# Three residual tiles, a root by logarithm and exponential, and a new order of projections in a two-layer graph attention kernel

## The reference

```python
h = relu(layernorm(x))                       # mean, variance, / sqrt(v + 1e-5)
q, k, v = h @ Wq + bq, h @ Wk + bk, h @ Wv + bv          # 16 heads of 32
attn = softmax(where(adj == 0, -inf, q k^T / sqrt(32)))   # per head
x = x + (attn @ v) @ Wo + bo
h = relu(layernorm(x))
alpha = (h @ wq) (h @ wk)^T                  # one head of 512
alpha = softmax(max(alpha, 0) * (adj != 0), axis=queries)
x = x + alpha @ (h @ weight)
```

## Time and profile before

| | |
|---|---|
| median of 3 runs | 1922.6 us (1919.81 to 1924.29) |
| the profiled execution | 1918.12 us, its span 1916.3 us, mean granted TensorE clock 0.99 |
| PE busy | 1779.5 us, 93% of the span |
| PEld busy | 1404.2 us, 73% |
| DVE busy | 1620.9 us, 85% |
| ACT busy | 1087.8 us, 57% |
| POOL busy | 452.0 us, 24% |
| DMA | 142.48 MB, mean 74 GB/s |
| chain that ended last, by engine | PE 50%, DVE 28%, issue 8%, DMA 6%, ACT 5% |

### The profile page before, as it was taken

How to read it: one execution, slowest core, us unless ns; L and a number is a source line. 1 busy time by engine, 2 the same in 40 slices (tenths; PEclk the granted TensorE clock), 3 DMA queues, 4 the chain that set the end, 5 groups by cost and what they waited for, 6 DMA issues and landing times.

```text
span 1916.3 us, 53466 instructions
## 1 busy us (share of the span) xinstructions
PE 1779.5 (93%) x16817; PEld 1404.2 (73%) x16817; DVE 1620.9 (85%) x4904; ACT 1087.8 (57%) x2381; POOL 452.0 (24%) x1190
## 2 busy tenths in 40 slices
PE   3789999999999999999999999999999999999986
PEld 2557777777777777777777777777777777777763
DVE  5688888988888898888888888888888888888884
ACT  2356555656565555656566565656565656656551
POOL 1022221222122222222122222212221222222111
PEclk9899999999999999999999999999999999999998
DMA  3412122222222222222222221222222222222121
GB/s 109 139 53 77 50 84 81 81 70 78 74 58 80 84 69 78 79 59 74 79 86 67 79 79 51 82 82 71 79 79 68 65 78 85 68 79 79 44 58 39
DMA packets 195401, 142.48 MB, mean 74 GB/s; under 512 B 36000, under 2 KB 167072, under 8 KB 195360
## 3 DMA queue, kind: packets, MB, share of 16 engines
q1 hardware_dynamic: 178224, 108.93, 19.9%
q10 hardware_dynamic: 17136, 33.03, 5.5%
HBM read 57.94 MB, written 16.78 MB: 39 GB/s over the span
## 4 chain that ended last, share of the span: by engine, by line
PE 50%; DVE 28%; issue 8%; DMA 6%; ACT 5%; SPq 1%; ACTq 1%; DVEq 1%; POOL 0%; POOLq 0%
PE ring L360 34%; PE turned L425 6%; DVE probs L792 6%; DMA out_dram<-x 5%; ACT probs L588 3%; PE score L410 3%; DVE probs_t_lo L800 3%; DVE x L930 2%; DVE val L891 2%; PE ring L478 2%; PE pv L443 2%; DVE work L859 2%; DVE o_sum L813 2%; DVE xa L859 2%; DVE e_lo L951 1%
## 5 line engine op out<-in xcount | busy, mean ns | idle before, releaser
L598 ACT ACTIVATE probs_t_hi<-turned 128x512 f16<-128x512 f32 x512 | 304.7, 595 | 371.5 <-PE turned L425 336.9
L588 ACT ACTIVATE probs<-probs,least 128x256 f32<-128x256 f32 x1024 | 461.3, 503 | 10.8 <-DVE least L792 10.8
L792 DVE CUSTOM_DVE_ANT_0 probs<-score,far,undo_score 128x256 f32<-128x256 f32 x1024 | 450.5, 478 | 9.6 <-DVE far L978 9.6
L1081 POOL TENSOR_TENSOR heads_out<-o_sum,o_rcp 128x64 f32<-128x64 f32 x512 | 144.6, 303 | 1150.3 <-DVE o_sum L813 1141.1
L800 DVE TENSOR_TENSOR probs_t_lo<-turned,probs_t_hi 128x512 f16<-128x512 f32 x512 | 350.3, 684 | 50.8 <-ACT probs_t_hi L598 47.3
L425 PE MATMUL turned<-ident,probs 128*128 128x128 f32 x2048 | 311.6, 275 | 42.7 <-ACT probs L588 42.7
L425 PEld LDWEIGHTS turned<-ident,probs 128*128 128x128 f32 x2048 | 244.6, 142 | 89.1 <-ACT probs L588 53.3
L410 PE MATMUL score<-stack 128*128 128x256 f16 x1024 | 197.1, 274 | 16.4 <-DMA stack<-stage 16.4
L443 PE MATMUL pv<-val,probs_t_hi 128*128 128x65 f16 x2048 | 184.7, 191 | 4.6 <-DVE o_sum L813 2.7
L445 PE MATMUL pv<-val,probs_t_lo 128*128 128x33 f16 x2048 | 178.2, 179 | 0.0
L443 PEld LDWEIGHTS pv<-val,probs_t_hi 128*128 128x128 f16 x2048 | 157.8, 97 | 11.7 <-DVE probs_t_lo L800 5.6
(11 more groups left out here) (160 smaller groups left out, 4307.8 us busy)
## 6 DMA issues: line engine op xcount, KB each, us to landing
stack<-stage SPq DMA_DIRECT2D x2048, 32.0 KB, 1.9
x<-x_dram ACTq DMA_DIRECT2D x32, 512.0 KB, 4.4
out_dram<-x SPq DMA_DIRECT2D x32, 512.0 KB, 2.9
xa<-x_dram ACTq DMA_DIRECT2D x31, 512.0 KB, 3.7
adj_in<-adj_dram SPq DMA_DIRECT2D x32, 256.0 KB, 2.9
adjt_in<-adj_t_dram SPq DMA_DIRECT2D x32, 256.0 KB, 3.0
wq_raw<-wq_dram SPq DMA_DIRECT2D x2, 512.0 KB, 6.2
wk_raw<-wk_dram SPq DMA_DIRECT2D x2, 512.0 KB, 7.9
```

The source lines that it names most:

```text
L588: last = nc.scalar.activation(probs[:, u % 2, q, :], probs[:, u % 2, q, :], ACT.Exp, bias=least[:, u % 2, q:q + 1], scale=-1.0)
L598: nc.scalar.activation(pH[:, u % 2, :, :], turned[u % 2][:].rearrange("p (k n) -> p k n", k=QT), ACT.Copy).then_inc(hi["p"], 1)
L792: last = nc.vector.tensor_tensor_reduce(out=probs[:, u % 2, q, :], in0=score[u % 2][:, q * NODES:(q + 1) * NODES], in1=far[:, q, :], scale ...
L1081: last = nc.gpsimd.tensor_tensor(dst, o_sum[:, pair % 2, q:q + 3:2, :], o_rcp[:, pair % 2, q:q + 3:2].unsqueeze(2).broadcast_to([P, 2, HEAD]),
```

## The change

- `xin` and `xo` join `x1`: ScalarE loads x of graph t into `xin` at the head of step 4 of body t; GpSimd adds the bias from `xin` into `x1` in step 1 of the next body, after the outputs of the graph before are made; VectorE adds the second layer's product from `x1` into `xo`; the store reads `xo`. SyncE issues the store a body later, between stacks 2 and 3, and the last one at the end.
- The second norm's root is made by ScalarE as exp(-0.5 ln(v + eps) + ln ROOT), and VectorE applies one Newton step, folded into three operations. The variance is aggregated right after step 4's turned low part. ScalarE asks for one activation table set at its start.
- The first norm's normalisation moves from VectorE to GpSimd, as (x + minus_mean) * rstd, with one small operation more for minus_mean; its first statistics move from step 7 to 8.
- The second softmax's low part moves from the head of step 13 to behind the mask of step 12. The last pair's sum goes ahead of step 0's turned low part.
- In the dense table `qk1` (next graph) comes in steps 11 and 13, `v0` in steps 14 and 15. Stack 1 of the next graph is issued right after its stack 0.

The diff, without the new tiles' and semaphores' declarations and with most unchanged lines left out:

```diff
@@ -19 +21 @@
-NSTEPS = (3 + 4 * NEWTON_ROUNDS, 2 + 3 * NEWTON_ROUNDS)
+NSTEPS = (4 + 4 * NEWTON_ROUNDS, 3)
+ROOT = 0.5 ** (1.0 / 3.0)
@@ -35 +38 @@
     ["al"],
-    ["v0a"],
+    ["qk1a"],
     ["hw1"],
-    ["v0b", "av0"],
-    ["av1", "qk1a"],
-    ["ot0", "qk1b"],
+    ["qk1b", "av0"],
+    ["v0a", "av1"],
+    ["v0b", "ot0"],
 ]
@@ -70 +73 @@
-STATS1, VAR1, NORM1 = (7, 9), 9, 12
+STATS1, VAR1, NORM1 = (8, 9), 9, 12
 VAR2, NORM2 = 4, 5
-X1_STEP, KEEP_STEP, FAR_STEP = 1, 3, 10
+X1_STEP, XIN_STEP, KEEP_STEP, FAR_STEP = 1, 4, 3, 10
@@ -162 +165 @@
         x1 = sb("x1", [P, QT, DIM], f32)
+        xin = sb("xin", [P, QT, DIM], f32)
+        xo = sb("xo", [P, QT, DIM], f32)
         adj_in = sb("adj_in", [P, QT, NODES], i32)
@@ -331 +340 @@
                 if cur:
-                    stack_heads(1, t)
                     stack_heads(2, t)
+                if prev and started(p - 1):
+                    store(p - 1)
+                if cur:
                     stack_heads(3, t)
...
                     stack_heads(0, n)
+                    stack_heads(1, n)
                 if nxt and not cur:
...
                             load_raw(sp, name, half)
-                if prev:
-                    sp.wait_ge(final, count(p, 2, 1))
-                    sp.dma_start(out_v[p, :, :, :], x1[:]).then_inc(stored, 16)
+            def store(b):
+                sp.wait_ge(final, count(b, 2, 1))
+                sp.dma_start(out_v[b, :, :, :], xo[:]).then_inc(stored, 16)
             sweep(sp, body)
+            store(BATCH - 1)
             sp.wait_ge(stored, 16 * BATCH)
@@ -573 +587 @@
         def _(act):
+            nc.scalar.preload_act_table_set("natural_log_exp_and_others")
             def split_high(c):
@@ -656 +672 @@
+            def root(b):
+                act.wait_ge(var_ok[1], count(b, 1, 0))
+                nc.scalar.activation(newton[1][:, 0, :], meanvar[1][:, :, 1], ACT.Ln,
+                                     bias=eps[:, 0:1]).then_inc(logged, 1)
+                act.wait_ge(logged, count(b, 1, 0))
+                nc.scalar.activation(rstd[1][:], newton[1][:, 0, :], ACT.Exp,
+                                     bias=log_root[:, 0:1], scale=-0.5).then_inc(rooted, 1)
             def second_softmax(s, b):
@@ -678 +702 @@
                 present = {-1: prev, 0: cur, 1: nxt}
-                if prev:
-                    if started(p - 1):
-                        act.wait_ge(stored, count(p - 1, 16, 15))
-                    act.dma_start(x1[:], x_v[p, :, :, :]).then_inc(x1_in, 16)
                 for s in range(HEADS):
+                    if cur and s == XIN_STEP:
+                        if prev:
+                            act.wait_ge(x1_ok, count(p, 1, 0))
+                        act.dma_start(xin[:], x_v[t, :, :, :]).then_inc(x1_in, 16)
                     if cur:
...
                         exponentials(0, t + 1)
+                    if s == VAR2 and prev:
+                        root(p)
                     if prev:
@@ -708 +734 @@
+            act.wait_ge(const_ok, 2)
             sweep(act, body)
@@ -831 +858 @@
...
+                y, a, c = rstd[1][:], newton[1][:, 1, :], newton[1][:, 2, :]
+                def step(ins, at):
                     ins.then_inc(nstep[1], 1)
+                    if at < NSTEPS[1] - 1:
+                        dve.wait_ge(nstep[1], count(b, NSTEPS[1], at))
+                dve.wait_ge(rooted, count(b, 1, 0))
+                step(nc.vector.scalar_tensor_tensor(out=a, in0=y, scalar=-1.0, in1=y,
+                                                    op0=ALU.mult, op1=ALU.mult), 0)
+                step(nc.vector.scalar_tensor_tensor(out=c, in0=meanvar[1][:, :, 1], scalar=EPS,
+                                                    in1=a, op0=ALU.add, op1=ALU.mult), 1)
+                step(nc.vector.scalar_tensor_tensor(out=y, in0=c, scalar=1.5 / ROOT, in1=y,
+                                                    op0=ALU.add, op1=ALU.mult), 2)
+            def second_normalise(b):
+                dve.wait_ge(nstep[1], count(b, NSTEPS[1], NSTEPS[1] - 1))
                 for q in range(QT):
+                    nc.vector.tensor_scalar(work[:, q, :], x1[:, q, :], meanvar[1][:, q, 0:1],
+                                            rstd[1][:, q:q + 1], ALU.subtract, ALU.mult
+                                            ).then_inc(normed[1], 1)
@@ -927 +947 @@
                     dve.wait_ge(mm["av"], count(b, 2, k))
-                    nc.vector.scalar_tensor_tensor(out=x1[:, k, :], in0=src[:],
+                    if k == 0 and started(b - 1):
+                        dve.wait_ge(stored, count(b - 1, 16, 15))
+                    nc.vector.scalar_tensor_tensor(out=xo[:, k, :], in0=src[:],
                                                    scalar=undo_final[:, 0:1], in1=x1[:, k, :],
@@ -945 +967 @@
                     nc.vector.reciprocal(l1_rcp[:], l1_sum[:]).then_inc(l1_rcped, 1)
-                if s == AL_STEP + 3:
...
+            def second_low(b):
+                dve.wait_ge(hi["e"], count(b, 1, 0))
+                for m in range(QT):
+                    last = nc.vector.scalar_tensor_tensor(
+                        out=eL[:, m, :], in0=work[:, 1, m * NODES:(m + 1) * NODES],
+                        scalar=l1_rcp[:, m:m + 1], in1=eH[:, m, :],
+                        op0=ALU.mult, op1=ALU.subtract)
+                last.then_inc(lo["e"], 1)
...
                     if prev and s == NORM2:
-                        normalise(1, x1, work, p)
+                        second_normalise(p)
                     if prev:
                         second_softmax(s, p)
+                    if s == 0 and prev:
+                        sum_parts(HEADS // 2 - 1, p)
                     if cur:
                         turned_low(s, t)
-                    if s == 0 and prev:
-                        sum_parts(HEADS // 2 - 1, p)
-                    elif s > 0 and s % 2 == 0 and cur:
+                    if s == VAR2 and prev:
+                        aggregate(1, p)
+                    if s > 0 and s % 2 == 0 and cur:
                         sum_parts(s // 2 - 1, t)
@@ -978 +1003 @@
                     if s == VAR2 and prev:
-                        aggregate(1, p)
                         reciprocal_deviation(p)
+                    if s == AL_STEP + 2 and prev:
+                        second_low(p)
                     if s in STATS1 and later:
                         first_stats(STATS1.index(s), n + 1)
-                    if s == NORM1 and cur and later:
-                        normalise(0, xa, xa, n + 1)
                     for name in DENSE[s]:
@@ -1003 +1027 @@
                             split_low(c)
-                if later and not cur:
-                    normalise(0, xa, xa, n + 1)
             for q in range(QT):
...
             step(nc.vector.memset(top[:], 0.0))
+            nc.vector.memset(eps[:], EPS).then_inc(const_ok, 1)
+            nc.vector.memset(log_root[:], math.log(ROOT)).then_inc(const_ok, 1)
             dve.wait_ge(small_in, 64)
@@ -1032 +1055 @@
             step(nc.vector.memset(tops[:], 0.0))
-            normalise(0, xa, xa, 0)
             for c in range(FIRST):
@@ -1060 +1082 @@
                 settle(pool, pool_settled)
+                step(nc.gpsimd.tensor_scalar(minus_mean[:], meanvar[0][:, :, 0], -1.0, None,
+                                             ALU.mult))
                 step(nc.gpsimd.tensor_scalar(v, meanvar[0][:, :, 1], EPS, None, ALU.add))
@@ -1069 +1093 @@
                     step(nc.gpsimd.tensor_tensor(y, y, a, ALU.mult))
+            def first_normalise(b):
+                pool.wait_ge(nstep[0], count(b, NSTEPS[0], NSTEPS[0] - 1))
+                settle(pool, pool_settled)
+                for q in range(QT):
+                    nc.gpsimd.tensor_scalar(xa[:, q, :], xa[:, q, :], minus_mean[:, q:q + 1],
+                                            rstd[0][:, q:q + 1], ALU.add, ALU.mult
+                                            ).then_inc(normed[0], 1)
@@ -1093 +1125 @@
                         norm_heads(s // 2 - 1, t)
+                    if s == NORM1 and later:
+                        first_normalise(n + 1)
                     if s == X1_STEP and prev and not started(p - 1):
...
                     if s == X1_STEP and prev:
+                        if started(p - 1):
+                            pool.wait_ge(final, count(p - 1, 2, 1))
                         pool.wait_ge(x1_in, count(p, 16, 15))
                         for q in range(QT):
-                            last = nc.gpsimd.tensor_tensor(x1[:, q, :], x1[:, q, :], out_bias[:],
+                            last = nc.gpsimd.tensor_tensor(x1[:, q, :], xin[:, q, :], out_bias[:],
                                                            ALU.add)
@@ -1121 +1157 @@
             reciprocal_deviation(0)
+            first_normalise(0)
             sweep(pool, body)
```

(29 more changed lines are left out.)

10 lines of the change are left out of this document (removed).

## The result

The changed kernel takes 1848.4 us in the median of 4 runs (1848.08 to 1853.79), against 1923.1 us for the kernel before (4 runs, 1919.81 to 1924.29). The ratio is 0.962, with a 95% interval of 0.960 to 0.964. The direction was right; the size was not.

The account below looks back on a forecast made before the run. TensorE was taken as the bound, idle 2.00 us a graph; 1.59 a graph times 30 is 47.7, plus 3.8 at the tail and 0 at the start, 51.5: 1866.6, given as 1870 by the median, range 1856 to 1895.

Parts of the forecast that it names:

- head, less the new wait: Steps 0 and 1: TensorE's wait for ScalarE's exponential, 1.24 us a graph, goes entirely; 0.22 is lost again.
- the new wait: Head of a graph: third group's product waits for the values' low part, now in step 15; 0.22 us a graph lost.
- first norm's transposes: Step 6: TensorE's wait for the values' low part, 0.51 us a graph, shrinks by 0.45 through the new root.
- last product: Step 13: second softmax's low part made a step earlier, so TensorE's 0.12 us wait a graph goes.
- the sign "under 0.1": Step 6: if the forecast is right, the xa transposes' wait falls under 0.1 us a graph.
- The root: Steps 4 and 5: VectorE's 11 Newton operations become 3, 2.08 against 0.57 us; ScalarE's two activations, 0.3 each, are free.
- The rival of table loads: ScalarE's root: two table loads of 1.28 us each time, 0.5 us a graph lost, 1905 us; chance 0.05.
- the third rival: Steps 12 and 13: GpSimd's normalisation blocks VectorE throughout, 1.2 us a graph lost, 1954 us by the median; chance 0.04.
- The start: First graphs: TensorE's stand for a stack moves to head 8, some 14 us, clock falls; gain 0, between -4 and +5.
- The tail: Program's end: 3.8 us gained, from the addition 1.6, the Newton chain 0.8, the earlier low parts 1.0 and 0.4.
- The offset: Whole kernel: 1866.6 us for a profiled execution, given as 1870 because the median of the runs lay 4.5 higher.
- the forecast's own range: Whole kernel: 1861 to 1884 us, from a residual of 0.2 to 0.8 a graph and -4 to +5 at the start.

Follow-up runs that it names:

- the first improvement: Changed kernel with VectorE's second normalisation moved from the head of step 5 into its idle time in step 4: 1833.38 us.
- the longer wait: Changed kernel with one more 128x512 copy on VectorE ahead of the values' low part in step 15: 1867.94 us.
- all three improvements: Changed kernel with second normalisation in step 4, both `v0` halves in step 14, last weights' loads ahead of the first stacks: 1812.68 us.

## Why the prediction was wrong

**The step that failed** is in its first part: "the most any reordering can win in the steady part is 2.00 us a graph". It read the ceiling from the idle column, and then priced each wait by its idle time. The account by graph, from starts of matmuls:

| | forecast | idle time gone | step length gone |
|---|---|---|---|
| head, less the new wait (steps 0, 1) | 1.02 | 1.24 - 0.19 | 1.31 |
| second norm's transposes (step 5) | none | 0.07 | 0.28 |
| first norm's transposes (step 6) | 0.45 | 0.24 | 0.24 |
| last product (step 13) | 0.12 | 0.12 | 0.26 |
| sum | 1.59 | 1.48 | 2.09 |

The first row holds the 1.67 of the head, less 0.36 for the new wait; 0.13 of it came by the moved sum. Times 30, 2.14 is 64 us, and 2.1 more lie in graph 2 alone (58.53 before, 54.30 after): from graph 1 to graph 31 the traces show 66.2 where 47.7 was forecast. That is 18.5 of the 21.6 us missed. A wait that is shortened (step 6, 0.66 to 0.41 above the pitch) gives back its idle time and no more; one that vanishes gives its fixed part too (steps 0 and 13). The runs bear this out one at a time: 0.50 for 0.27, 0.35 for 0.19, and 0.59 for 0.59 where nothing vanished.

**Step 6** came out as the forecast's chain said, and still left a wait. The values' low part was forecast for 940.2 on the clock of before. In the changed kernel it ends at 906.89 + 0.68 = 907.57, and step 5 begins 32.65 us earlier there (902.06 for 934.71): 940.22. But TensorE arrives 0.28 earlier, since the unlisted wait in step 5 is gone. The other 0.13 of the 0.41 that it stands there over the pitch were in the forecast's own rows: it let TensorE arrive at 940.39, the listed end of the last matmul, where the pitch gives 940.24, and start with the low part's end, where it starts 0.15 later. So the sign "under 0.1" for this wait failed, at 0.27.

```profile
906.89 0.68 DVE L911 TENSOR_TENSOR val<-ring,val 128x512 f16<-128x512 f32 x1
```

**The root** went as forecast: two activations of 0.30 each (0.3 assumed), then VectorE's three, done at 902.63; and then VectorE stands idle for ScalarE.

```profile
901.02 0.30 ACT L677 ACTIVATE newton<-meanvar,eps 128x2 f32<-128x2 f32 x1 [0.43 <-DVE meanvar L850]
901.35 0.30 ACT L680 ACTIVATE rstd<-newton,log_root 128x2 f32<-128x2 f32 x1
...
902.91 0.47 ACT L643 ACTIVATE stage<-ring,bias_q 128x256 f16<-128x256 f32 x1 [1.27 <-PE score L424]
```

```profile
902.47 0.16 DVE L873 SCALAR_TENSOR_TENSOR rstd<-newton,rstd 128x2 f32<-128x2 f32 x1
903.78 0.48 DVE L902 SCALAR_TENSOR_TENSOR stage<-ring,bias_q,stage 128x256 f16<-128x256 f32 x1 [1.16 <-ACT stage L645]
```

The rival of table loads is dead: the two activations stand 0.33 apart, with no load between them, and the group of table loads holds one in the whole execution:

```profile
L590 ACT ACT_TABLE_LOAD x1 | 1.3, 1283 | 0.7 <-PEq L1185 0.7
```

The 1.16 us at 903.78 is what the forecast left lying, and the first improvement uses it.

**GpSimd** was costed at 1.7 us for a 128x512 normalisation. It takes 0.76:

```profile
929.42 2.14 POOL L1155 TENSOR_SCALAR far_next<-adj_in 128x256 bf16<-128x256 int32 x2
931.53 0.81 POOL L1113 TENSOR_TENSOR heads_out<-o_sum,o_rcp 128x64 f32<-128x64 f32 x2
932.33 1.51 POOL L1101 TENSOR_SCALAR xa<-xa,minus_mean,rstd 128x512 f32<-128x512 f32 x2
```

The rows it was estimated from were a two-operand addition (1.27) and a conversion from int32, and neither is near. VectorE's low part beside it took 0.88 for two, as before, while GpSimd's scaling took 0.81 where it takes 0.54 alone:

```profile
931.06 0.88 DVE L974 SCALAR_TENSOR_TENSOR e_lo<-work,l_rcp,e_hi 128x256 f16<-128x256 f32 x2
```

So GpSimd waits and VectorE does not, in this pairing: the third rival falls. The Trainium skill ("SBUF — State Buffer", on the shared port pair) lets whoever starts first have the ports, and the other blocks until it is through. The trace agrees for the scaling, which started second and took longer. It does not agree for the low part, which started at 931.06 while GpSimd's conversion ran until 931.56, and took 0.48 for the first half (0.47 in the kernel before) and not 0.5 more. With the softmax's low part given back to step 13 it does meet GpSimd's normalisation: VectorE's two then took 0.94, and GpSimd's two 1.93 in place of 1.51. GpSimd paid the most there too, and VectorE 0.06.

```profile
990.88 0.94 DVE L974 SCALAR_TENSOR_TENSOR e_lo<-work,l_rcp,e_hi 128x256 f16<-128x256 f32 x2
```

```profile
990.37 1.93 POOL L1101 TENSOR_SCALAR xa<-xa,minus_mean,rstd 128x512 f32<-128x512 f32 x2
```

**The start** came out as worked out. The stand moved from head 4 to head 8:

```profile
77.38 0.61 PE L424 MATMUL score<-stack 128*128 128x256 f16 x2 [10.95 <-DMA stack<-stage]
...
70.00:80.00 10.00, 2.62 (x19) 2.50 (x20) 3.29 (x9) 0.60 (x1) 0.54 (x2) 0.53 0.57 164
```

It is 10.95 us where 14 was said, ends at 77.4 where 75.4 was said, and the clock is granted at 0.53 in the ten microseconds around it, close to the lower level of 1.2 GHz. The gain up to step 13 of graph 1 is 0.9 us, inside -4 to +5; in the changed kernel's second profile it is -1.2, so it can't be told from nothing.

**The tail** was said to give 3.8 and gave 2.3: 0.74 in step 13 of the last graph (1.0 forecast) and 1.6 behind it (2.8). Its last 24 output products took 7.03 us where the kernel before took 5.64. The stretch from 1807 to 1815 is granted 0.79; the kernel before has 1.00 in 1875 to 1882. The fall is not a property of the changed tail: the same products took 6.50 in its second profile, and 5.64 in that of the longer wait, whose tail has the same code. So 1.4 of the 1.5 us missed here came with the execution that was profiled. Why the clock falls in one and not in another stays open.

```profile
1808.31 0.63 PE L374 MATMUL ring<-wo_lo,heads_t_hi 128*128 128x512 f16 x1
1808.73 0.63 PE L374 MATMUL ring<-wo_hi,heads_t_lo 128*128 128x512 f16 x1
```

**The offset.** The profiled execution of before lay 4.5 us under the median, and 3.4 of that went into the forecast. That of after lies at its median (1848.75 and 1848.43), so those 3.4 us were error too.

**The range.** By its own terms (0.2 to 0.8 a graph, -4 to +5 at the start) the forecast's own range is 1859 to 1886, not 1861 to 1884. That changes nothing: 1848.4 lies outside either.

## What to carry to other kernels

Price a wait of TensorE from start to start of its matmuls, less their usual pitch in a stream; the idle column leaves out the drain in front and the refill behind, here 0.15 to 0.25 us that are paid once per wait, and waits of 0.07 and 0.12 us of idle, or of none, are in no table. So look for starts that come later than the pitch, and for an end on another engine 0.15 us before them; count a ceiling from the pitch; taking away the last 0.2 us of a wait is worth more than the first. When one tile holds a store, a load and the work of an in-order engine together, free the tile before its queue is given more to issue.

## What the runs showed of the hardware

- TensorE starts 0.14 to 0.15 us after the end of the VectorE or GpSimd operation that it waited for (0.10 behind the softmax's low part), also where the wait shows no idle time: 32 of 32 graphs in the run with all three improvements (937.37 and 937.51).
- VectorE's two-input low part keeps its 0.48 us although GpSimd's conversion is running when it starts; GpSimd's scaling beside it goes from 0.54 to 0.81, its normalisation from 1.51 to 1.93.
- GpSimd's (x + a) * b with two per-partition operands takes 0.76 us for 128x512 float32, its addition of two full tensors 1.27 and its conversion of half as many int32 elements 1.07. No run separates the number of tensors from the kind of operation.
- ScalarE's 128x2 logarithm and exponential take 0.30 us each and need one table load in the whole execution, though exponential, logarithm, copy and relu take turns in every graph.
- TensorE's busy time is no constant of the work: 54.44, 53.84 and 53.49 us a graph for the same matmuls, the less it waits the less it is "busy".
